# Tiles of the experts begin before the last batch's attention tail, whose pieces run between their products

## The chip, the cores and the metric

One core of one Trainium2 chip runs the whole kernel. The metric is the device time of one execution in microseconds. TensorE (PE) multiplies, VectorE (DVE) and ScalarE (ACT) do the elementwise work, GpSimd (POOL) does some of it and issues the indirect DMAs, SyncE (SP) issues the plain DMAs. Each engine runs its own program in order; they meet at semaphores.

## What is computed

8 batches of 512 tokens, width 256. Two layers, each followed by a layer norm over the sum with its input:

```
qkv = x @ qkv_w.T + qkv_b            # 16 heads of 16, causal softmax, attn @ v
mem_score ...                        # a decayed cumulative memory of 6x6 outer products per head
x1 = layernorm(x + (seq_out + gated * mem_val) @ out_w.T + out_b)
logits = x1 @ wr + br                # 4 experts, the best 2 per token
h = gelu(x1 @ w1[e] + b1[e]);  y = h @ w2[e] + b2[e]        # 256 -> 1024 -> 256
c[e] = gelu(b1[e]) @ w2[e] + b2[e];  c_sum = c.sum(experts)
out = layernorm(x1 + sum_k gate_k * (y[e_k] - c[e_k] + c_sum))
```

So a token's expert rows need only that token's x1 and routing; the constant rows c need weights alone.

## The kernel before, in words

**Attention.** `schedule` (L351) runs steps 0 to 9. In step i the scores, values and memory of batch i-1 run, the queries of batch i+1, and the tail of batch i-2: o_tokens, z, z_rows, projection, layernorm, seed, normalise, x1_rows, logits, gates, rank. Within a step every engine walks the same list of about 190 stage names, `stages_of_a_step` (L46), an order written out by hand, and does its own part of each stage. Step 8 (`B`) has no new queries, step 9 (`B + 1`) is the tail of the last batch alone. After `rank` POOL scatters each token's row of x1 (with its token number, its two gates and its expert) into `slots`, a region in DRAM for each expert, by 8 indirect DMAs a batch (L742). SP stores x1 in `sums` (L531).

**Weights of the experts.** 16 chunks of 128x1024 f32 come by 8 DMAs of 1 MB (L465). `weights(n)` turns a chunk into two f16 halves: ACT copies the high one (L805), DVE forms the low one (L1318). Chunks 0 to 5 are converted in step 8, chunks 6 to 15 in step 9.

**Constants.** In step 9 PE multiplies gelu(b1) with the f16 halves of w2 (`expert_of_nothing`, L1175, 96 matmuls); behind it DVE forms `c_all`, `c_sum` and `base` (L1631 to L1639).

**Table.** When all batches are ranked, DVE works out a table of 35 tiles of 256 rows (L1583 to L1626, some 40 small operations, most waiting for the one before): for each tile its expert, its first row in `slots` and how many rows to leave out. SP waits for all scatters and the table, then loads the rows of tiles 0 and 1.

**Tiles.** `ffn_schedule` (L364) runs tiles 0 to 35. In tile t PE does, for hc = 0 to 7, `first_layer(hc)` of tile t (6 matmuls, L1220) and `second_layer(hc)` of tile t-1 (6 matmuls, L1231); after hc 3 it transposes the rows of tile t+1 (`rows_of`, 4 transposes, L1208). ACT applies gelu (L949) and copies the transposed rows (`rows_high`, L940). DVE makes two f16 halves of each hidden block (L1681, L1683), at hc 4 the low half of the next tile's rows (`rows_low`, L1657), at hc 5 the bias (L1653), at hc 6 the gates (L1666 to L1674), and after hc 7 scales the output rows of tile t-1 (L1697, L1703), which POOL adds into `sums` (L767). `first_layer(hc)` waits for the gelu of four blocks before, a gelu for DVE's halves of four blocks before that; and PE may not begin tile t+1 before DVE has done `rows_low(t + 1)`, which stands behind hc 4 of tile t on DVE.

**End.** SP loads `sums`, DVE, ACT and POOL normalise, SP stores.

Of the kernel before, what the change touches and what calls it, by code (L numbers as in the profile page):

```python
# [13 lines left out]
P = 128  # L14
# [21 lines left out]
TABLE = TILES + 2  # L36
REGION = ROWS + N
# [4 lines left out]
RAW_B = range(4, 10)  # L42
# [69 lines left out]
def attention_and_ffn(nc, x_tok, x_tr, w_proj, qk_bias, v_bias, mem_bias, gate_bias, mem_scale, iter_mix, decay_logits, w_out,  # L112
                      out_bias, w_route, b_route, w_1, b_1, w_2, b_2, out):
    ctx = ExitStack()
    with ctx:
        sb = lambda name, shape, dt: ctx.enter_context(nc.sbuf_tensor(name, shape, dt))
        ps = lambda name: ctx.enter_context(nc.psum_tensor(name, [P, 512], F32))
        sem = lambda name: ctx.enter_context(nc.semaphore(name))
        dram = lambda name, shape, dt: nc.dram_tensor(name, shape, dt, kind="Internal").ap()


        q_rows = dram("q_rows", (2, 33, NP2, T), F16)
        k_rows = dram("k_rows", (2, 33, NP2, T), F16)
        decay_rows = dram("decay_rows", (H, 3 * P), F32)
        slots = dram("slots", (E * REGION, ROW), F32)
        sums = dram("sums", (N + ROWS, D), F32)


        def carve(arena, at, shape, dt):
# [31 lines left out]
        qk_parts, at = carve(arena_b, at, (4, 2, T), F16)  # L161
        v_aug, at = carve(arena_b, at, (C, H, 32), F32)
# [6 lines left out]
        w_raw_b, after_raw = carve(arena_b, after_probs, (len(RAW_B), CHUNK), F32)  # L169

        def raw_chunks(n, m=1):

            return w_raw_b[:, n - RAW_B[0]:n - RAW_B[0] + m, :] if n in RAW_B else w_raw[:, n:n + m, :]


        g_hi, g_lo, xt_hi, xt_lo, rows_x, y_out = ([None, None] for _ in range(6))
        at = 0
        for n in range(2):
            g_hi[n], at = carve(arena_b, at, (HC, ROWS), F16)
            g_lo[n], at = carve(arena_b, at, (HC, ROWS), F16)  # L180
# [173 lines left out]

        block = ctx.enter_context(nc.Block())

        stages = stages_of_a_step()

        def run(mine, i, ab, c, t):

# [66 lines left out]
        def _(sp):  # L427
# [80 lines left out]
            def step(i, par, ab, c, t):  # L508
# [32 lines left out]
                if ab:  # L541
# [3 lines left out]
                    if not later(i, 1):  # L545
                        tables()
# [1243 lines left out]
```

## Time and profile before

| what | us |
|---|---|
| runs | 1074.76, 1075.88 (median), 1081.32 |
| profiled execution, its own time | 1073.04 |
| its span, first to last instruction | 1071.3 |
| one attention step, from the stage table (steps 2, 4 and 5) | 68 |
| last matmul of the attention's values | 590.6 |
| first matmul of tile 0 | 640.81 |
| last matmul of the tiles | 1026.4 |
| busy PE, DVE, ACT, POOL | 938.2, 831.6, 490.4, 427.0 |

The times in rows are us from the start of the span. Matmuls are pipelined: in a run of them the start of the next is the better measure of what one costs than its own duration.

### The profile page before, as it was taken

The page shows a single profiled execution, that of the slowest core. Times are in us where ns is not written, and L with a number is a line of the kernel's source. Part 1 is how long each engine was busy: PE and PEld are TensorE (multiplying, and loading weights), DVE is VectorE, ACT ScalarE, POOL GpSimd, SP SyncE. Part 2 cuts the span into 40 slices and gives each one's busy share as a digit, 9 for nine tenths or more (in the row PEclk, how much of TensorE's full clock was granted, in tenths as well). Part 3 has the DMA queues.
Part 4 walks back from the last instruction along what each step waited for, and adds up shares of the span by engine and source line. Part 5 has one row for each costly group of instructions (what it writes and reads, how often), then busy time and mean ns, then how long its engine had stood idle before and what let it go on. Part 6 is the DMA issues. An engine that isn't in the chain of part 4 may idle for free.

```text
span 1071.3 us, 28021 instructions
## 1 busy us (share of the span) xinstructions
PE 938.2 (88%) x8034; PEld 688.5 (64%) x8035; DVE 831.6 (78%) x2944; ACT 490.4 (46%) x1038; POOL 427.0 (40%) x371
## 2 busy tenths in 40 slices
PE   4699999998999999998988749999999999999930
PEld 1155656565566565655645538888989889898920
DVE  4658798896988988978878867777777777777737
ACT  4174654554545555554555514333343334333304
POOL 8336084453553735636356131232323223232321
PEclk9699999999999999999999869999999999999975
DMA  4662124132032140320341311233332323232357
GB/s 161 180 179 71 32 62 120 41 91 94 22 110 91 60 121 1 105 76 21 125 192 41 118 61 32 41 55 44 50 48 49 49 49 49 49 49 42 53 114 234
DMA packets 60073, 85.19 MB, mean 80 GB/s; under 512 B 8473, under 2 KB 50985, under 8 KB 58953
## 3 DMA queue, kind: packets, MB, share of 16 engines
q1 hardware_dynamic: 45680, 62.20, 19.6%
q0 software_dynamic: 14304, 21.90, 11.1%
q8 instruction: 45, 0.74, 0.3%
q14 instruction: 44, 0.35, 0.1%
HBM read 48.08 MB, written 35.86 MB: 78 GB/s over the span
## 4 chain that ended last, share of the span: by engine, by line
PE 65%; DVE 17%; DMA 5%; issue 5%; SPq 2%; ACT 2%; POOL 2%; DVEq 1%; ACTq 0%; POOLq 0%
PE st L1220 8%; PE sm L1220 8%; PE pv L1231 8%; PE sm L1231 8%; PE ms L995 6%; PE sm L1077 5%; PE st L1037 4%; PE pv L1057 4%; DVE junk L1446 3%; PE ms L1135 3%; DVE beaten L1393 2%; PE ms L1107 2%; PE st L1039 2%; PE ms L1119 2%; PE ms L1208 2%
## 5 line engine op out<-in xcount | busy, mean ns | idle before, releaser
L1446 DVE CUSTOM_DVE_ANT_0 junk<-sm,mask_ts 128x512 bf16<-128x512 f32 (+3 forms) x512 | 220.3, 486 | 59.4 <-PE sm L1077 57.0
L885 ACT ACTIVATE arena_b<-st 128x512 f32<-128x512 f32 x320 | 181.7, 598 | 112.4 <-PE st L1039 111.1
L767 POOL DMA_INDIRECT sums<-arena_b x70 | 111.2, 1588 | 290.8 <-DVE arena_b L1703 253.0
L1037 PE MATMUL st<-arena_a 128*128 128x384 f16 (+3 forms) x512 | 127.8, 306 | 19.5 <-ACT arena_b L885 10.6
L1077 PE MATMUL sm<-arena_a 128*128 128x512 f16 (+3 forms) x512 | 115.2, 312 | 20.5 <-DVE maxes L1446 12.6
L1683 DVE TENSOR_TENSOR arena_b<-arena_b 128x256 f16<-128x256 f32 x280 | 119.7, 428 | 9.6
L949 ACT ACTIVATE arena_b<-st,arena_b 128x256 f32<-128x256 f32 x140 | 66.3, 473 | 116.7 <-PE st L1220 105.9
L949 ACT ACTIVATE arena_b<-sm,arena_b 128x256 f32<-128x256 f32 x140 | 66.3, 474 | 115.1 <-PE sm L1220 81.6
L1681 DVE CAST arena_b<-arena_b 128x256 f16<-128x256 f32 x280 | 87.7, 313 | 40.3 <-ACT arena_b L949 38.0
L1220 PE MATMUL st<-arena_b,arena_a 128*128 128x256 f16 x840 | 115.6, 275 | 1.8 <-DVE arena_b L1657 1.8
L1231 PE MATMUL pv<-arena_a,arena_b 128*128 x864 | 116.8, 273 | 0.0
L1220 PE MATMUL sm<-arena_b,arena_a 128*128 128x256 f16 x840 | 115.1, 274 | 0.0
L1231 PE MATMUL sm<-arena_a,arena_b 128*128 x816 | 111.3, 273 | 0.0
L742 POOL DMA_INDIRECT slots<-res,slot_i x64 | 65.8, 1028 | 105.9 <-DVE slot_i L1435 88.9
L1037 PEld LDWEIGHTS st<-arena_a 128*128 128x128 f16 x512 | 50.6, 99 | 74.5 <-ACT arena_b L885 27.5
L1039 PE MATMUL st<-mask_st,ident_b 128*128 128x128 bf16 x512 | 96.0, 221 | 0.0
L1231 PEld LDWEIGHTS pv<-arena_a,arena_b 128*128 128x128 f16 x864 | 84.4, 98 | 10.0
L1220 PEld LDWEIGHTS st<-arena_b,arena_a 128*128 x840 | 82.4, 98 | 12.2 <-issue 2.5
L1220 PEld LDWEIGHTS sm<-arena_b,arena_a 128*128 x840 | 82.6, 98 | 10.1
L1057 PE MATMUL pv<-arena_b 128*32 128x512 f32 (+3 forms) x1024 | 88.5, 447 | 0.0
L1231 PEld LDWEIGHTS sm<-arena_a,arena_b 128*128 128x128 f16 x816 | 79.8, 98 | 9.3
L1077 PEld LDWEIGHTS sm<-arena_a 128*128 128x128 f16 x512 | 41.8, 100 | 67.6 <-DVE maxes L1446 36.3
(253 smaller groups left out, 1657.1 us busy)
## 6 DMA issues: line engine op xcount, KB each, us to landing
arena_b<-slots SPq DMA_DIRECT2D x37, 260.0 KB, 2.7
arena_a<-w SPq DMA_DIRECT2D x5, 1024.0 KB, 8.5
arena_b<-x_tr SPq DMA_DIRECT2D x8, 512.0 KB, 3.7
q_rows<-arena_b SPq DMA_DIRECT2D x32, 128.0 KB
k_rows<-arena_b SPq DMA_DIRECT2D x32, 128.0 KB
arena_a<-q_rows SPq DMA_DIRECT2D x32, 128.0 KB
arena_a<-k_rows SPq DMA_DIRECT2D x32, 128.0 KB
res<-x_tok POOLq DMA_DIRECT2D x8, 512.0 KB, 4.0
```

Source lines behind the costliest of these rows:

```text
L767: pool.indirect_dma_start(sums, bass.IndirectOffsetOnAxis(ap=token_now[:, 1 - par, m:m + 1], axis=0), y_out[1 - par][:, m, :], None, compu ...
L885: act.activation(probs[:, q, :], st_ps[piece % 2][:, :], ACT.Exp, scale=SCORE_SCALE).then_inc(exp_done, 1)
L949: act.activation(g_32[:, hc % 4, :], u_bank(hc)[:, 0:ROWS], ACT.Gelu, bias=b1_now[:, par, hc:hc + 1], scale=1.0 / W_SCALE).then_inc(gelu_d ...
L1037: pe.matmul(out[:, at:at + width], ks[:, h % 2, h // 2, s * P:(s + 1) * P], qs[:, h // 2, s * P:T], start=m == 0, stop=False, skip_group_c ...
L1039: last = pe.matmul(out[:, at:at + P], ident_b[:, :], mask_st[:, :], start=False, stop=True, skip_group_check=True)
L1057: last = pe.matmul(out[32 * hl:32 * hl + 32, s * P:T], v_aug[:, s, 4 * g + hl, :], probs[:, slot, col:col + width], start=cls == 0, stop=c ...
L1077: last = pe.matmul(sm_ps[n % 3][:, at:at + width], qs[:, j, tile * P:(tile + 1) * P], ks[:, p, j, 0:width], start=m == 0, stop=True, skip_ ...
L1220: last = pe.matmul(u_bank(hc)[:, 0:ROWS], w_by_expert[:, up_expert, at:at + P], xs[par][:, kc, :], start=kc == 0 and n == 0, stop=kc == KC ...
L1231: last = pe.matmul(y_ps[1 - par][:, m * D:(m + 1) * D], gs[1 - par][:, hc, m * P:(m + 1) * P], w_by_expert[:, down_expert, at + lo * CHUNK ...
L1446: last = dve.tensor_tensor_reduce(junk[:, n % 3, at:at + width], sm_ps[n % 3][:, at:at + width], mask_ts[:, T - width:T], 1.0, NEG, ALU.ad ...
L1681: dve.tensor_copy(g_hi[par][:, hc, :], g_32[:, hc % 4, :]).then_inc(ghi_done, 1)
L1683: dve.tensor_tensor(g_lo[par][:, hc, :], g_32[:, hc % 4, :], g_hi[par][:, hc, :], ALU.subtract).then_inc(hid_done, 1)
```

## The change

- `stages_of_a_step` loses `weights`, `last_memory_scores` and step 9's four `nothing`, gains `load_w2`, `nothing`, `first_expert` and `first_rows`, and some 14 other stages stand one or two places from where they stood. Step 9 is no longer a step.
- Step 9's stages are dealt out by hand (`stages_of_the_tail`): two places in each of tiles 0 to 20. PE does its part after hc 1 and hc 5, ACT and DVE after hc 3 and hc 7, SP and POOL once a tile. All of the tail's PE stages use the one bank `ms1`.
- Constants: in step 0 ACT issues 8 DMAs (4 MB) of raw w2; in step 1 PE multiplies them in f32 with gelu(b1), 32 matmuls of 32 columns by 256, into `pv` (before the values), ACT copies, SP writes 4 rows to DRAM; in step 8 they are read back, and POOL forms `base` (5 operations) before the tiles.
- The table is made in three parts: 6 tiles in step 7 (`first_expert`: the most loaded expert after six batches has at least 1536 tokens, 6 tiles), tiles 6 to 24 in tiles 0 to 2 from the counts of seven batches, tiles 25 to 36 in tiles 18 to 20 from all counts. Experts are numbered from the most loaded one on, and their weights are fetched in that order.
- Weights: chunks 0 to 3 in step 8, chunks 4 to 15 in tiles 1 to 5. SP loads chunks 14, 15, 10 to 13 in step 8, chunks 4, 5 before tile 0, 6 to 9 in tiles 0 and 1.
- In step 0 SP sends the decays and the row of maxima before the rows of batch 1, where it sent them after.

```diff
+EARLY = (2 * (N - T) - E * (ROWS - 1) + ROWS - 1) // ROWS      # 25
+LATE = TABLE - EARLY                                           # 12
+UNROLLED = EARLY - 2                                           # 23
+SURE = 2 * (N - 2 * T) // E // ROWS                            # 6
...
+    tail = {
+        (0, 0): [("load_weights", 3)], (0, 1): [("early_table", 0)],
+        (1, 0): [("load_weights", 4), ("weights", 4), ("early_table", 1)], (1, 1): [("weights", 5)],
+        (2, 0): [("weights", 6), ("early_table", 2)], (2, 1): [("weights", 7), ("weights", 8)],
+        (3, 0): [("weights", 9), ("weights", 10)], (3, 1): [("weights", 11)],
+        (4, 0): [("weights", 12), ("weights", 13)], (4, 1): [("weights", 14)],
+        (5, 0): [("weights", 15)], (5, 1): [("last_memory_scores", 0)],
+        (6, 0): [("o_tokens", 0)], (6, 1): [("o_tokens", 1), ("last_memory_gates", 0)],
+        (7, 0): [("o_tokens", 2), ("last_gates", 0)], (7, 1): [("o_tokens", 3), ("z", 0)],
+        (8, 0): [("z_rows", 0), ("z", 1)], (8, 1): [("z_rows", 1), ("z", 2)],
+        (9, 0): [("z_rows", 2), ("z", 3)], (9, 1): [("z_rows", 3)],
+        (10, 0): [("projection", 0)], (10, 1): [("projection", 1)],
+        (11, 0): [("projection", 2)], (11, 1): [("projection", 3)],
+        (12, 0): [("layernorm", 0)], (12, 1): [("layernorm", 1)],
+        (13, 0): [("seed", 0)], (13, 1): [("layernorm", 2), ("layernorm", 3)],
+        (14, 0): [("normalise", 0), ("normalise", 1)], (14, 1): [("normalise", 2), ("normalise", 3)],
+        (15, 0): [("x1_rows", 0), ("store", 0)], (15, 1): [("x1_rows", 1)],
+        (16, 0): [("x1_rows", 2)], (16, 1): [("x1_rows", 3)],
+        (17, 0): [("logits", 0)], (17, 1): [("gates", 0)],
+        (18, 0): [("rank", 0)], (18, 1): [("late_table", 0), ("scatter", 0)],
+        (19, 0): [("late_table", 1)], (19, 1): [("late_table", 2)], (20, 0): [("late_table", 3)], (20, 1): [("late_table", 4)],
+    }
...
-            step(B + 1, 1, False, False, True)
-        def ffn_schedule(eng, tile):
-            tile(0, 0, True, False)
-            tile(1, 1, True, True)
-            tile(2, 0, True, True)
-            with eng.Fori(0, (TILES - 3) // 2) as k:
+        def tail(mine, t, point):
+            for stage, n in tail_stages.get((t, point), ()) if isinstance(t, int) else ():
+                if stage in mine:
+                    mine[stage](n)
+        def ffn_schedule(eng, tile, before_late):
+            for t in range(UNROLLED):
+                tile(t, t % 2, True, t > 0)
+            before_late()
+            with eng.Fori(0, (TILES - UNROLLED) // 2) as k:
...
+            def base_of_experts():                       # POOL, ahead of the tiles
+                pool.wait_ge(base_in, 32)
+                pool.tensor_tensor(b2_all, b2_all, base, ALU.add).then_inc(base_chain, 1)
+                for e in range(1, E):
+                    pool.wait_ge(base_chain, e)
+                    pool.tensor_tensor(c_sum, b2_all[:, 0, :] if e == 1 else c_sum, b2_all[:, e, :], ALU.add).then_inc(base_chain, 1)
+                pool.wait_ge(base_chain, E)
+                pool.tensor_tensor(base, c_sum.unsqueeze(1).broadcast_to([P, E, D]), base, ALU.subtract).then_inc(base_done, 1)
...
+            def load_w2(_):                              # ACT, step 0
+                act.wait_ge(rows_in[0], 16 * N_ROWS_IN)
+                for e in range(E):
+                    for n in range(2):
+                        act.dma_start(w2_raw[2 * e + n], w_2[e, :, n, :].rearrange("p (a t) -> p a t", a=2)).then_inc(w2_in, 16)
...
+                    pe.wait_ge(w2_in, 32 * E)            # PE, step 1, behind ("scores", 3)
+                    pe.wait_ge(gb_done, 1)
+                    pe.wait_ge(bias_done, 1)
+                    for hc in range(HC):
+                        for e in range(E):
+                            rows = w2_raw[2 * e + hc // 4][:, hc % 4 // 2, D * (hc % 2):D * (hc % 2) + D]
+                            last = pe.matmul(pv_ps[32 * e:32 * e + 32, 0:D], gb[:, HC * e + hc:HC * e + hc + 1].broadcast_to([P, 32]), rows,
+                                             start=hc == 0, stop=hc == HC - 1, skip_group_check=True)
...
+                if isinstance(i, int) and i == B + 1:    # PE: bank()
+                        n = 1
...
                 if up:                                   # PE: tile()
                     pe.wait_ge(xt_lo_s, n_of(t + 1))
+                    if not later(t, 1):
+                        pe.wait_ge(wlo_done, CHUNKS)
+                    elif not later(t, SURE + 1) and later(t, SURE):
+                        pe.wait_ge(wlo_done, CHUNKS * E)
...
+                    if up and hc in (1, 5):
+                        tail(mine, t, hc // 4)
...
+            pe.wait_ge(table_done, 3)
+            pe.wait_ge(exp_done, 40 * B)
+            pe.wait_ge(mrow_done, 2 * B)
...
+                        if hc in (3, 7):                 # DVE and ACT: tile()
+                            tail(mine, t, hc // 4)
```

## Rows read from the trace of the kernel before

**Rows 1.** The page: busy us of each engine, share of the span, instructions.

```profile
PE 938.2 (88%) x8034; PEld 688.5 (64%) x8035; DVE 831.6 (78%) x2944; ACT 490.4 (46%) x1038; POOL 427.0 (40%) x371
```

**Rows 2.** Stage table: stretch, length, busy of PE, PEld, DVE, ACT, POOL, clock, DMA.

```profile
528.00:594.00 66.00, 55.34 (x484) 35.51 (x483) 54.84 (x163) 38.03 (x82) 36.38 (x29) 0.97 0.39 145
594.00:641.00 47.00, 26.13 (x163) 20.01 (x164) 35.19 (x112) 16.56 (x28) 10.11 (x9) 0.72 0.20 67
...
800.00:900.00 100.00, 100.00 (x918) 89.96 (x917) 76.80 (x257) 39.07 (x83) 28.64 (x18) 1.00 0.30 48
```

**Rows 3.** PE in order of time: start, length, line; last values, first tiles.

```profile
589.09 1.50 PE L1057 MATMUL pv<-arena_b 128*32 128x384 f32 x24
...
640.81 2.74 PE L1220 MATMUL st<-arena_b,arena_a 128*128 128x256 f16 x12 [1.61 <-DVE arena_b L1657]
...
665.98 0.60 PE L1208 MATMUL ms<-ident,arena_b 128*128 128x128 f32 x4
666.41 0.82 PE L1220 MATMUL st<-arena_b,arena_a 128*128 128x256 f16 x6
```

**Rows 4.** DVE groups, 700 to 1000 us: busy, mean ns, idle before and releasers.

```profile
L1681 DVE CAST arena_b<-arena_b 128x256 f16<-128x256 f32 x220 | 69.0, 314 | 28.6 <-ACT arena_b L949 26.9
...
L1653 DVE COPY arena_b<-b_all 128x8 f32 x28 | 4.9, 174 | 14.2 <-ACT arena_b L949 8.2 <-issue 5.9
```

**Rows 5.** In order of time: DVE's `rows_low(3)`, and PE's first matmul of tile 3.

```profile
668.45 0.68 DVE L1657 TENSOR_TENSOR arena_b<-ms,arena_b 128x512 f16<-128x512 f32 x1
...
671.65 0.82 PE L1220 MATMUL st<-arena_b,arena_a 128*128 128x256 f16 x6
```

**Rows 6.** DVE in order of time, 589 to 629 us: the tail's pieces.

```profile
589.45 0.56 DVE L1499 TENSOR_TENSOR mr<-rdm,lines 128x384 f32<-128x384 f32 x1
...
593.03 0.23 DVE L1519 TENSOR_SCALAR sg<-sg 128x128 f32<-128x128 f32 x1
...
593.80 0.25 DVE L1526 RECIPROCAL rec<-ms 128x16 f32<-128x16 f32 x1
...
596.58 0.22 DVE L1550 TENSOR_SCALAR sg<-sg 128x128 f32<-128x128 f32 x1
...
598.64 1.67 DVE L1538 SCALAR_TENSOR_TENSOR zs<-mv_odd,gated,zs 128x256 f32<-128x256 f32 x4
...
616.83 0.17 DVE L1388 TENSOR_TENSOR lg<-ms,b_r 128x16 f32<-128x16 f32 x1
...
620.59 0.17 DVE L1435 CAST slot_i<-slot_k 128x8 int32<-128x8 f32 x1
620.67 2.35 DVE L1318 SCALAR_TENSOR_TENSOR arena_a<-arena_a 128x1024 f16<-128x1024 f32 x2
622.95 0.16 DVE L1583 TENSOR_TENSOR count<-first_free,first_slot 128x4 f32<-128x4 f32 x1
...
628.87 0.24 DVE L1626 CAST arena_b<-arena_b 128x37 int32<-128x37 f32 x1
```

**Rows 7.** POOL, and DVE, in order of time: a DVE operation beside a POOL addition.

```profile
571.34 2.37 POOL L727 TENSOR_TENSOR mv_odd<-mv_odd,mem_b 128x1024 f32<-128x1024 f32 x1
...
571.41 2.32 DVE L1393 TENSOR_TENSOR beaten<-lg 128x8 f32<-128x8 f32 x1
```

**Rows 8.** ACT in order of time: the load of gelu's table.

```profile
620.99 1.28 ACT L934 ACT_TABLE_LOAD   x1
```

**Rows 9.** Chain of waits: start, us, what: PE's projection and logits of a tail.

```profile
503.61 1.75 PE ms L1152 x16
...
547.23 2.72 PE ms L1135 x12
```

**Rows 10.** PE in order of time: step 1's first scores; 8 matmuls of 32 columns.

```profile
53.91 0.61 PE L1037 MATMUL st<-arena_a 128*128 128x512 f16 x1 [4.29 <-DMA arena_a<-max_row]
...
563.06 0.64 PE L1057 MATMUL pv<-arena_b 128*32 128x256 f32 x8
```

**Rows 11.** The page's DMA issues: size, median us from issue to landing.

```profile
arena_a<-w SPq DMA_DIRECT2D x5, 1024.0 KB, 8.5
```

More of the change, by code:

```diff
@@ L529, in step @@
                     b = i - 2
[L530 to L531 removed]
+                    store(b, par)
+                if ab and not later(i, 1):
+                    decays_out()
+                    max_rows_in(i, par, 0)
+                    decays_in()
                 if ab and before_end(i, 1):
@@ L573, in tile, with before_late @@
                     sp.wait_ge(row_info, n_of(t + 1))
+                    if not later(t, SURE - 1) and later(t, SURE - 2):
+                        sp.wait_ge(scattered, 128 * (B - 1))
+                        sp.wait_ge(table_done, 6)
                     load_rows(t + 2, par)
-            load_rows(0, 0)
-            load_rows(1, 1)
-            ffn_schedule(sp, tile)
+                    tail(mine, t, 0)
+            def before_late():
+                sp.wait_ge(scattered, 128 * B)
+                sp.wait_ge(table_done, 9)
+            sp.wait_ge(st_ready, 40 * B)
+            load_weights(2)
+            mine = {"load_weights": load_weights, "store": lambda _: store(B - 1, 1)}
+            ffn_schedule(sp, tile, before_late)
             for n in range(2):
@@ L976, in queries_and_keys, with rows_of @@
                 last.then_inc(qk_ready, 1)
+            def rows_of(t, par):
+                if not later(t, 1):
+                    pe.wait_ge(cs_read, 6 * B - 1)
+                pe.wait_ge(rows_x_in[par], n_of(16 * half(t) + 16))
+                if later(t, 1):
+                    pe.wait_ge(xt_lo_s, n_of(t))
+                for kc in range(KC):
+                    for m in range(2):
+                        last = pe.transpose(ms_ps[0][:, kc * ROWS + m * P:kc * ROWS + (m + 1) * P], rows_x[par][:, m, kc * P:(kc + 1) * P], ident[:, :])
+                last.then_inc(xt_ready, 1)
             def step(i, par, ab, c, t):
@@ L1224, in second_layer @@
                 def second_layer(hc):
+                    if hc == 0 and not later(t, 2):
+                        pe.wait_ge(o_evac, 4 * B)
                     if hc == 0 and later(t, 3):
@@ new lines, in tiles_of, with starts_of @@
+            def tiles_of(out, rows, more_rows):
+                f(dve.tensor_scalar(n_tok, rows, more_rows, None, ALU.add))
+                f_wait()
+                f(dve.tensor_scalar(n_int, n_tok, ROWS.bit_length() - 1, None, ALU.arith_shift_right))
+                f_wait()
+                f(dve.tensor_copy(out, n_int))
+                f_wait()
+            def starts_of(tiles):
+                f(dve.memset(starts[:, 0:1], 0.0))
+                f(dve.tensor_copy(starts[:, 1:2], tiles[:, 0:1]))
+                f_wait()
+                for e in range(1, E):
+                    f(dve.tensor_tensor(starts[:, e + 1:e + 2], starts[:, e:e + 1], tiles[:, e:e + 1], ALU.add))
+                    f_wait()
@@ new lines, in by_position, with positions @@
+            def by_position(out, n, first, steps):
+                f(dve.tensor_scalar(out, past[:, 0, 0:n], steps[:, 0:1], first, ALU.mult, ALU.add))
+                f_wait()
+                for e in range(1, E - 1):
+                    f(dve.scalar_tensor_tensor(out, past[:, e, 0:n], steps[:, e:e + 1], out, ALU.mult, ALU.add))
+                    f_wait()
+            def positions(at, n, now):
+                for e in range(E - 1):
+                    f(dve.tensor_scalar(past[:, e, 0:n], now, starts[:, e + 1:e + 2], None, ALU.is_ge))
+                f_wait()
+                f(dve.tensor_tensor(tab_f[:, 3, at:at + n], past[:, 0, 0:n], past[:, 1, 0:n], ALU.add))
+                f_wait()
+                f(dve.tensor_tensor(tab_f[:, 3, at:at + n], tab_f[:, 3, at:at + n], past[:, 2, 0:n], ALU.add))
+                f_wait()
@@ L1689, in tile @@
                             row_gates()
+                        if hc == 3 and not later(t, SURE) and later(t, SURE - 1):
+                            dve.wait_ge(table_done, 6)
+                        if hc in (3, 7):
+                            tail(mine, t, hc // 4)
                 if down:
                     dve.wait_ge(y_ready, n_of(t))
+                    if not later(t, 2):
+                        dve.wait_ge(base_done, 1)
                     if later(t, 3):
```

462 lines of the change are left out of this document (289 added, 173 removed).

## The prediction

> **What bounds the kernel now.** I read the page's busy shares first: PE is busy 88% of the span, DVE 78%, so PE leads and DVE is close behind [rows 1]. The stage table says where PE isn't the bound: in the steady tiles PE is busy 100 of 100 us at the full clock of 2.4 GHz; between the attention and the tiles it is busy 26 of 47 us, at a granted clock of 0.72 [rows 2]. PE in order of time gives the edges of that stretch: the last values end at 590.6, tile 0 begins at 640.81 [rows 3]. In it stand the last tail (a chain from engine to engine), the conversion of ten weight chunks, the constants, the table, the last scatter and the first loads. This stretch is what the change opens. Then I asked the tiles how much room there is for what is put between them. A tile is 100 matmul records and 918 start in 100 us, so 10.9 us [rows 2]. DVE's idle time waiting for ACT is 26.9 + 8.2 us in 300 us, 27.5 tiles: 1.3 us a tile [rows 4]. The rest of what looks idle on DVE is issue of instructions (gaps ahead of the bias and of the output rows), shorter where tiles are written out, so I take 1.5 us of real room and 9.4 us of DVE work a tile. And the nearest deadline is tight: `rows_low(3)` ends at 669.13, PE begins tile 3 at 671.65 [rows 5]. DVE may be late by 2.5 us at that place; every further us holds PE.
>
> **The sum.** It starts at the profiled execution's own time, 1073.0; the median of the runs, 1075.9, lies 2.8 above it, and I add that at the end.
>
> *Tiles start earlier.* PE needs the last exponentials, the expert of tile 0 and the first four chunks, all of step 7 or 8, so tile 0 begins about 0.3 us behind the values: 590.9 for 640.81, -49.9.
>
> *Start-up of the tiles.* A group of four transposes holds PE for 0.43 (665.98 to 666.41, [rows 3]), so a group of six matmuls takes (10.9 - 0.43) / 16 = 0.65. From 640.81 the transposes inside tile 2 should come after 2.6 + 8.3 + 10.9 us, at 662.6; they stand at 665.98. The first 12 matmuls of tile 0 took 2.74 instead of 1.3 us, the half clock of 1.2 GHz behind a long gap; the rest was waits. With no gap both go: -3.3.
>
> *PE's share of the tail* now lies in the tiles, where PE is full, so it counts whole. 32 f32 transposes, 0.43 for four: 3.5. The projection, 16 matmuls at 2.72 for 12: 3.6; the logits 1.75 [rows 9]; rank 0.3. Together +9.1. The 96 matmuls of the constants are gone with the gap.
>
> *Tiles 0 to 5, DVE.* Prices [rows 6]: one low half of a chunk 2.35 / 2 = 1.17; the last memory scores 589.45 to 593.26, 3.8; a chained small operation: 5.92 us from 622.95 for about 33 rows, 0.18. The three early tables are about 12, 9 and 8 such operations, the first with a register load (one such gap is up to 0.6): 2.7, 1.9, 1.6. DVE's work is then, tile by tile: 7.8 (no output rows yet) + 2.7 = 10.5; 9.4 + 2.3 + 1.9 = 13.6; 9.4 + 3.5 + 1.6 = 14.5; 12.9; 12.9; 9.4 + 1.2 + 3.8 = 14.4. Sum 78.8. ACT first has to load gelu's table (1.28, [rows 8]), so DVE starts 2.4 us behind PE. `rows_low(6)` stands 8.9 us ahead of the end of that sum, so PE begins tile 6 at 2.4 + 78.8 - 8.9 = 72.3 us from the start of tile 0. PE alone would be there after 5.7 (tile 0 has a first layer only) + 5 x 10.9 = 60.2. **Stall: +12.1.** This is the largest term against the change: what hid DVE in the tiles was 1.5 us a tile, and 4.1 a tile are put on it.
>
> *Base on POOL.* Five additions, two of 1024 elements (2.37 each, [rows 7]) and three of 256, about 6.5 us around 595 to 602, in tiles 0 and 1. A DVE operation of 8 elements with both operands in SBUF took 2.32 beside such an addition [rows 7]; the tail's small ones, with POOL idle, take 0.16 to 0.25 [rows 6]. The halves L1681 and L1683 read and write SBUF, so they should be held too. Bounds: 0 to 6.5; as DVE is the bound there and still gets an operation in between, I take +4.5.
>
> *Tiles 6 to 8.* DVE comes into tile 6 late, and the tail's PE stages share one bank: `o_tokens(1)` (after hc 5) waits until DVE has read `o_tokens(0)` (after its hc 3). DVE is there at 81.2 (the whole sum) + 2.7 (four blocks) + 0.65 (reciprocal 0.25 and product 0.42, rows 6) = 84.6, PE at 72.3 + 0.4 + 8.3 = 81.0: 3.6. Tile 7 puts 0.65 + 2.06 (the gates, 596.58 to 598.64) and 1.05 on DVE; `z_rows(0)` comes another 0.5 late. +4, bounds 1 and 7. From tile 9 to 16 DVE's pieces are below 2 us a tile, and PE's own pieces give room: 0.
>
> *Tiles 17 to 21.* Logits and rank are 3.9 us on DVE (616.83 to 620.76, rows 6), in tiles that PE lengthens by 1.75. Then five parts of the late table, about 2.4, 1.6, 2.1, 1.9, 1.2, stand in two and a half tiles with 1.5 us of room each, plus the 2.5 of the deadline: +3, bounds 1 and 6.
>
> *ACT.* Three places need Exp or Ln between gelus, six table loads: 7.7 us at 1.28 [rows 8]. A pair (away from gelu and back) and its operations take about 3 us, and PE asks for that gelu four blocks later; at tile 13 the delayed `rows_high` just meets the deadline: 0, at most +2. The Trainium skill (ScalarE: Activation LUTs, What ACT_TABLE_LOAD costs) states that a switch costs as much again in a drain, 2.66 us; by that the pair would be 5.3 and tile 13 about 2.5 us late, and the sum 2.5 higher. The row's next operation starts 0.02 us behind the load, so the trace does not show the drain.
>
> *Steps 0 to 8.* The constants are 32 matmuls of 256 f32 columns, four side by side; 8 such held PE for 0.57 [rows 10], so 2.3 at full clock, 4.6 at half. They wait for 4 MB; 1 MB landed after 8.5 us [rows 11] and ACT issues them some 20 us ahead, beside the tiny row of maxima for which PE waited 4.29 us [rows 10]. That row is now sent about 1.5 us sooner. Net +1.5, bounds -1.5 and +8. `first_expert` puts about 16 chained operations on DVE in step 7, 3 us: +1, bounds 0 and 3. The moved stages: PE is not busy for 10.7 of the 66 us of step 8 [rows 2], so a better or worse order can give or take about 1 us a step; I take 0, bounds -4 and +4. The scatter (8 indirect DMAs on POOL in tile 18), the store and the row loads on SP have a tile or more of slack behind them: 0. Chunks 4 and 5 are issued behind 2 MB at 590 and wanted at 603: at most 8.5 each, in parallel, 0, bound +5.
>
> Sum: 1073.0 - 49.9 - 3.3 + 9.1 + 12.1 + 4.5 + 4 + 3 + 1.5 + 1 = **1055.0**, and with 2.8 **1057.8** as a median. Forecast: 1058.
>
> **Rivals.**
> *DVE takes it in.* If the small operations and gaps overlap when DVE runs behind, and POOL holds nothing, the 23.6 us of stalls shrink to 5: 1039. For it: no row shows DVE working off a backlog longer than one tile's end. Against it: a work sum of 78.8 us in 60 us leaves at least 12 less what overlaps. 12%.
> *The gain is spent on waits that I priced at nothing.* A stall of ACT for chunks 4 to 9 (SP may issue 6 and 7 only behind `row_info` of tile 1, then 8.5 us), the 4 MB in front of the row of maxima, a worse order. Price: 5 + 8 + 4 on top, 1065 to 1075, no change that can be told. 14%.
> *Slower: the clock falls with the stalls.* PE waits about 2.5 us at the head of each of tiles 1 to 8. In the gap of now the granted clock was 0.72 for a busy share of 26 in 47, in step 8, with 55 of 66 busy, 0.97 [rows 2]; tiles with 20% waiting lie like step 8. Were the clock at 1.2 GHz for all of tiles 0 to 8, their 93 us would be 186, less the 20 of stalls that this would hide: 1131. It takes about 36 us at half clock, beyond those that fill stalls, to lose the whole gain. 4%.
> *It doesn't start early.* SP's program of step 8 is one line of waits (constants written, scatters of six batches, table) ahead of the rows of tile 0; if one came late, tile 0 would wait. All of them are met by 575 to 580; each us late costs one us. 2%.
>
> **How the numbers follow.** My case, stalls of 14 to 32 us, has 68%: 1047 to 1067. The range goes down half way to the first rival and up to where the second has most of its weight: 1043 to 1072. What a measurement here can tell from no change is about 1%, 10.8 us: faster is below 1065.1. My case but its upper twelfth and the first rival make 0.74 for faster, the second rival and that twelfth 0.20, the clock and the rest 0.06.
>
> **What would show it.** The trace of after should have the first L1220-like matmul near 591; PE waits for `rows_low` (DVE) at the head of tiles 1 to 6, about 2 us each; DVE busy over 90% from 593 to 670 with f16 halves stretched to 2 us around 598; tile 6 near 668; waits of the tail's transposes for DVE in tiles 6 and 7; free running from 9 to 17; a few us of waits in 19 to 21. The term most likely off is POOL's. If DVE turns out to run below 90% in tiles 1 to 5 while PE waits, another engine or a load is late and my mechanism is wrong.

## The result

| | median us | runs | ratio to the kernel before, 95% interval |
|---|---|---|---|
| before | 1077.38 | 4 | |
| changed | 1065.18 | 4 | 0.988 [0.985, 0.991] |
| changed, measured again | 1061.14 | 5 | 0.983 [0.981, 0.986] |

The forecast was 1058, range 1043 to 1072. The change makes the kernel 1.2 to 1.7% faster, its time is 7 us above the forecast in the first series and 3 in the second, in which the kernel before had 1078.09 (9 runs). The profiled execution of the changed kernel took 1066.83, its span is 1065.1.

The page of the changed kernel, busy us of each engine, answers to [rows 1]: PE has 9 us less than before (the constants alone are busy for 5.1 us instead of 12.4), DVE 3 us more.

```profile
PE 929.2 (87%) x8002; PEld 676.0 (63%) x8003; DVE 835.0 (78%) x2990; ACT 495.6 (47%) x1045; POOL 430.5 (40%) x376
```

The stage table of the changed kernel, columns as in [rows 2]:

```profile
528.00:594.00 66.00, 56.20 (x490) 34.90 (x490) 51.92 (x160) 36.75 (x82) 33.82 (x28) 0.97 0.29 101
594.00:641.00 47.00, 40.47 (x353) 33.08 (x352) 37.11 (x114) 23.12 (x44) 16.72 (x14) 0.93 0.45 152
641.00:700.00 59.00, 53.74 (x470) 46.43 (x468) 53.24 (x156) 28.90 (x52) 16.40 (x10) 0.97 0.29 46
800.00:900.00 100.00, 95.23 (x869) 84.49 (x867) 79.91 (x305) 38.73 (x80) 36.00 (x26) 1.00 0.34 63
```

Between 594 and 641 PE now does 40.5 us of work instead of 26.1: the gap is full. But from 641 to 700 it is busy for only 53.7 of 59 us, and DVE for 53.2, that is 90%. The steady tiles of [rows 2], 100 of 100, have become 95 of 100 where pieces of the tail lie between them.

PE in order of time (the number in brackets is its idle time ahead and what ended it), the end of the attention and the head of tiles 0 and 1; it answers to [rows 3]:

```profile
599.77 1.50 PE L1222 MATMUL pv<-arena_b 128*32 128x384 f32 x24
...
601.45 1.48 PE L1375 MATMUL st<-arena_b,arena_a 128*128 128x256 f16 x12 [0.17 <-issue]
...
604.08 0.60 PE L1138 MATMUL ms<-ident,arena_b 128*128 128x128 f32 x4
...
612.46 1.46 PE L1375 MATMUL st<-arena_b,arena_a 128*128 128x256 f16 x6 [5.16 <-DVE arena_b L1659]
613.71 1.49 PE L1388 MATMUL pv<-arena_a,arena_b 128*128 x6
...
616.27 1.49 PE L1388 MATMUL pv<-arena_a,arena_b 128*128 x6
617.55 0.96 PE L1375 MATMUL sm<-arena_b,arena_a 128*128 128x256 f16 x6
618.35 0.82 PE L1388 MATMUL pv<-arena_a,arena_b 128*128 x6
...
696.67 0.60 PE L1138 MATMUL ms<-ident,arena_b 128*128 128x128 f32 x4
```

Tile 0 starts 0.2 us behind the last values, at 601.45 instead of 640.81. Then tile 1's first product waits 5.16 us for `rows_low(1)`. Behind that wait six matmuls take 1.46 to 1.49 us instead of 0.82: the engine is back at 1.2 GHz for four groups (the granted clock from 609 to 620 is 0.69). Their pitch is 1.28 instead of 0.65, so the wait costs 2.5 us more than its length.

What PE waited for between 594 and 860, in the changed kernel (us in total, times, longest):

```profile
PE ms L1138 <- DMA arena_b<-slots: 7.2, 8, 1.9
PE st L1375 <- DVE arena_b L1659: 6.9, 3, 5.2
PE ms L1284 <- DVE zs L1862: 2.4, 1, 2.4
```

The forecast had only the second and third. The first is the load of a tile's rows; whether it is a cause of its own is what one of the experiments asks. DVE and POOL behind tile 0, the lines that answer to [rows 7]:

```profile
602.37 2.35 POOL L798 TENSOR_TENSOR arena_b<-arena_b 128x1024 f32<-128x1024 f32 x1
604.80 2.39 POOL L801 TENSOR_TENSOR arena_b<-arena_b 128x256 f32<-128x256 f32 x3
607.27 2.40 POOL L803 TENSOR_TENSOR arena_b<-arena_b 128x1024 f32<-128x1024 f32 x1
```

```profile
603.85 1.03 DVE L1940 CAST arena_b<-arena_b 128x256 f16<-128x256 f32 x1 [3.87 <-ACT arena_b L1099]
...
607.40 2.42 DVE L1940 CAST arena_b<-arena_b 128x256 f16<-128x256 f32 x1
609.86 0.42 DVE L1942 TENSOR_TENSOR arena_b<-arena_b 128x256 f16<-128x256 f32 x1
610.20 0.29 DVE L1940 CAST arena_b<-arena_b 128x256 f16<-128x256 f32 x1
```

A cast of 0.29 us takes 2.42 beside POOL's last addition. The first three blocks take 603.85 to 610.20, 6.35 us, where three free ones take 2.0.

**Four lengths** serve for all comparisons below, since a start that is late by chance drops out of them. *Step 1*: from the first to the second transposes of maxima. *Attention*: from the first of these to the end of the last values. *Tiles 1 to 8*: from the transposes inside tile 0 to those inside tile 7 (604.08 to 696.67 here, 92.6; free of waits and of the tail's pieces it would be 73.8, since half of the first of these seven spans belongs to tile 0, which has no second layer: 8.3, then six times 10.9). The *tile phase* runs from tile 0's first product to the end of the last first-layer product.

| us | step 1 | attention | tiles 1 to 8 | tile phase |
|---|---|---|---|---|
| before, its two traces | 32.0, 35.1 | 542.0, 545.3 | 75.1, 75.1 | 379.7, 379.6 |
| changed, its two traces | 38.3, 36.7 | 549.6, 550.2 | 92.6, 92.4 | 411.7, 409.6 |

### The profile page after: what moved, and what is told of

Its sections match the earlier page's. It is cut to its first block, busy times and chain, and to the rows that moved or that the text cites. A ratio compares the mean times of both kernels' runs of the same rounds, so it can differ in the third digit from the quotient of the medians.

```text
span 1065.1 us, 26698 instructions
## 1 busy us (share of the span) xinstructions
PE 929.2 (87%) x8002; PEld 676.0 (63%) x8003; DVE 835.0 (78%) x2990; ACT 495.6 (47%) x1045; POOL 430.5 (40%) x376
## 4 chain that ended last, share of the span: by engine, by line
PE 55%; DVE 25%; issue 6%; DMA 6%; SPq 4%; ACT 2%; DVEq 1%; POOL 0%; ACTq 0%; POOLq 0%
PE sm L1375 6%; PE st L1375 5%; PE ms L1160 5%; PE sm L1388 5%; PE pv L1388 5%; PE sm L1242 5%; PE st L1202 4%; PE pv L1222 4%; DVE junk L1780 4%; PE ms L1300 3%; DVE arena_b L1942 3%; DVE arena_b L1940 2%; PE ms L1272 2%; DVE beaten L1727 2%; PE st L1204 2%
## 5 line engine op out<-in xcount | busy, mean ns | idle before, releaser
L1242 PE MATMUL sm<-arena_a 128*128 128x512 f16 (+3 forms) x512 | 112.9, 309 | 18.0 <-DVE maxes L1780 11.9
L792 POOL DMA_INDIRECT slots<-res,slot_i x64 | 62.5, 977 | 80.2 <-DVE slot_i L1769 62.8
L1242 PEld LDWEIGHTS sm<-arena_a 128*128 128x128 f16 x512 | 41.6, 99 | 63.1 <-DVE maxes L1780 35.1
```

The source lines that it names most:

```text
L1242: last = pe.matmul(sm_ps[n % 3][:, at:at + width], qs[:, j, tile * P:(tile + 1) * P], ks[:, p, j, 0:width], start=m == 0, stop=True, skip_ ...
```

## The experiments

**The control.** The changed kernel, no edit.

> The changed kernel as it is, as the measure for the three that run beside it. 1065 us, within 0.3%. Its trace of before the experiments has: values end at 601.3 us, tile 0's first product at 601.45, 25 us of waits of PE in the tiles. If the step markers (end of the last maxima of each step) stand at other places than 124.7, 193.6, 265.3, ..., part of the 8 us by which steps 0 and 1 came later is scatter between executions.

Measured: 1061.14 (5 runs), span 1064.0. The values end at 602.51, tile 0's first product is at 602.69. The marker of step 1 stands at 89.0 here and at 90.0 in the other trace, so most of the lateness stays, and where it stands moves by a microsecond or two between executions.

**The kernel before, once more,** to see how far its start moves.

> The kernel before, unchanged, for a second trace of it. The first transposes of maxima stood at 48.6 in its first trace and at 47.1, 47.7, 48.5, 51.0, 51.5, 51.6, 51.7, 52.3 and 52.5 in nine traces of the changed kernel and its variants. If that is scatter of the start in both kernels, this one stands anywhere between 47 and 53; if the changed kernel starts later as such, at 48.6 or less.

Measured: 1079.34. The lines of its trace for the two marks of step 1 and for tile 0's first product:

```profile
50.67 0.60 PE L1092 MATMUL sm<-ident,maxes 128*16 128x128 f32 x2 [1.40 <-DVE maxes L1446]
...
85.76 0.39 PE L1092 MATMUL sm<-ident,maxes 128*16 128x128 f32 x2 [0.44 <-DVE maxes L1446]
...
647.25 2.74 PE L1220 MATMUL st<-arena_b,arena_a 128*128 128x256 f16 x12 [1.61 <-DVE arena_b L1657]
```

The start is scatter in both kernels, up to 5 us between executions. The trace from which I forecast was an early one: tile 0 stood at 640.81 in it, at 647.25 in this one. The tile phase is the same to 0.1 us (379.7, 379.6).

**The tail in front of the tiles.** All five engines run the pieces of the tail before tile 0:

```
 def ffn_schedule(eng, tile, before_late, mine={}):
+    for at in sorted(tail_stages):
+        for stage, n in tail_stages[at]:
+            if stage in mine:
+                mine[stage](n)
```

> All pieces of the last batch's tail, the remaining conversions and the tables are run before tile 0 instead of between the products of tiles 0 to 20; nothing else is changed. It undoes the one part that the forecast makes the gain of. Theory: tile 0's first product starts 40 to 50 us later than 601, at 643 to 652; in the tiles DVE and PE have no extra work, so the 25 us of waits and the 9 us of PE's pieces go; 1065 + 45 - 25 - 9 = about 1076, no better than the kernel before. Rival (the earlier tiles are not worth their price, most of the gain over the kernel before comes from the other edits): below 1066.

Measured: 1115.19. PE in order of time:

```profile
666.59 3.55 PE L1319 MATMUL ms<-w_r,z_t 128*128 128x4 f32 x16 [0.56 <-ACT z_t L1010]
671.46 0.20 PE L1328 MATMUL ms<-taken,before 128*128 128x16 bf16 x1 [1.32 <-DVE taken L1734]
...
671.70 2.52 PE L1377 MATMUL st<-arena_b,arena_a 128*128 128x256 f16 x11
...
687.69 1.46 PE L1377 MATMUL st<-arena_b,arena_a 128*128 128x256 f16 x6 [8.44 <-DVE arena_b L1661]
...
1061.80 0.82 PE L1377 MATMUL sm<-arena_b,arena_a 128*128 128x256 f16 x6
```

Tile 0 starts at 671.70, 69 us later than the control's, not 40 to 50: the tail works with one bank of PSUM here, and DVE converts all twelve chunks before it (of PE's 45 us of waits, 29.5 are one wait for DVE). The tile phase is 390.9, 18.7 us shorter than the control's. It has a stall of its own at its head: DVE is still at the ranks and the late table when PE begins tile 0, and PE waits 8.4 us for `rows_low(1)`. From the transposes inside tile 1 to the end of the phase it takes 367.5, where the control takes 390.8 and the kernel before 365.5. So both halves of the trade are shown: between the products the pieces cost the tiles 19 us in all and 23 from tile 1 on, and not having them in front is worth more, 50 us less in the whole span of the two traces. The two sizes are those of this arrangement of the tail, which is worse than that of the kernel before with its gap of 50 us.

**POOL's additions moved into step 8.**

```
 (POOL, step 8)
+    if isinstance(i, int) and i == B:
+        base_of_experts()
     scatter(i, par)
 (POOL, behind step 8)
-    base_of_experts()
```

> The five additions for the base are moved on POOL from behind the scatter of step 8 (602.4 to 609.7) into POOL's idle time ahead of it (585.0 to 592.4); nothing else is changed. Theory (POOL's additions hold DVE's operations with SBUF operands, and DVE's lateness in tiles 0 to 5 passes to PE one for one): DVE's first three blocks take 2.0 us instead of 6.35, PE's waits in tiles 0 to 5 fall from 13.4 to about 9, and the kernel is 3.5 to 4.5 us faster than the control. Rival A (PE in tiles 2 to 5 waits for row loads and ACT, not for DVE's sum of work): the gap at tile 1 closes and comes back by tile 6, 0 to 1 us faster. Rival B: in step 8 the additions hold DVE's choice of experts or the memory's products instead; then the values end later than 601.3 by 2 to 4 us and the gain is gone.

Measured: 1062.53, ratio 0.986 [0.983, 0.988], no better than the control. Its trace shows why: tiles 1 to 8 take 86.3 (control 92.4), tile phase 404.2 (409.6), but from the transposes of maxima in step 8 to the last values it takes 41.0 instead of 37.2. Rival B: 5.4 us gained in the tiles, 3.8 lost in step 8. One line of DVE and one of POOL of this kernel:

```profile
586.39 1.95 DVE L1733 TENSOR_SCALAR taken<-place 128x16 bf16<-128x16 f32 x1
```

```profile
585.97 2.34 POOL L798 TENSOR_TENSOR arena_b<-arena_b 128x1024 f32<-128x1024 f32 x1
```

In the control that operation takes 0.17. It stands in the chain that chooses the experts, for which the memory's products wait.

**The base on 128 x 8 elements.** SP loads the rows of the constants spread over all partitions, POOL adds there, SP writes the base out and loads it broadcast in step 8:

```
+for q in range(E):
+    for to, of in ((small_b, b_2), (small_c, c_rows)):
+        sp.dma_start(to[32*q:32*q+32], AP(of, ap=[[8, 32], [D, E], [1, 8]]))   # end of step 6
-pool.tensor_tensor(b2_all, b2_all, base, ALU.add)        # 128x1024
+pool.tensor_tensor(small_b, small_b, small_c, ALU.add)   # 128x32, step 7
...
+sp.dma_start(base_rows, small_own)                       # step 8, then one broadcast load
```

> The base is computed in step 7 on 128 partitions x 8 elements (five additions of 8 to 32 elements instead of 256 to 1024), written to DRAM and loaded broadcast in step 8, so POOL adds nothing at 602 to 610 and nothing extra in step 8. Theory (moving the additions into step 8 gained 5.4 us in the tiles and lost 3.8 in step 8, because they held DVE there): now the 5.4 to 6 us of tile 1 are gained and step 8 stays at 37.2 us from its last transposes of maxima to the last values; tile phase 404 us, end 5 us earlier. Rival (step 8 in the moved kernel was longer by scatter or by something else than POOL's additions): step 8 is longer here too.

Measured: 1053.46 in one run. POOL and PE of this kernel:

```profile
511.46 0.26 POOL L813 TENSOR_TENSOR small_b<-small_b,small_c 128x32 f32<-128x32 f32 x1
511.80 0.76 POOL L816 TENSOR_TENSOR small_b<-small_b 128x8 f32<-128x8 f32 x3
512.64 0.20 POOL L818 TENSOR_TENSOR small_own<-small_b,small_own 128x8 f32<-128x8 f32 x1
```

```profile
604.03 0.83 PE L1391 MATMUL st<-arena_b,arena_a 128*128 128x256 f16 x6 [0.79 <-DVE arena_b L1675]
...
686.01 0.60 PE L1154 MATMUL ms<-ident,arena_b 128*128 128x128 f32 x4
```

The wait at tile 1 falls from 5.16 to 0.79 and the six matmuls behind it take 0.83: no half clock. Tiles 1 to 8 take 86.0 (600.02 to 686.01), the tile phase 402.4, and the last part of step 8 stays at 37.0. The term that I called "base on POOL" is 6.4 to 7.2 us: 4.4 of held DVE, and the rest mostly the clock behind the wait. The whole time of this single run is flattered by an early start (its first mark stands at 48.5).

**DVE without the low halves of chunks 4 to 15.**

```
+if n >= CHUNKS:
+    dve.memset(w_ffn[:, at + CHUNK:at + 2 * CHUNK].bitcast(F32), 0.0)
+    return
 dve.scalar_tensor_tensor(w_ffn[:, at + CHUNK:at + 2 * CHUNK], ...)
```

> DVE clears the low halves of chunks 4 to 15 instead of computing them (the products of the other experts lack that part): 12 instructions of 1.22 us become 12 of some 0.3, so DVE has 11 us less in tiles 1 to 5, all else alike. Theory (DVE's sum of work sets PE's waits in tiles 0 to 5): DVE's work per tile falls to about 10 to 11.5, PE's waits in tiles 0 to 8 fall from 18.0 to 7 or 8, 9 to 11 us faster than the control. Rival (row loads, issued by SP only after DVE's gates of the rows at the end of a tile and landing some us later, or ACT): waits for rows stay as they are, 3 us faster or less.

Measured: 1055.6 (6 runs), ratio 0.981 [0.978, 0.983]. DVE's groups between 605 and 690, of the changed kernel and of this one (instructions | busy us, mean ns):

```profile
L1485 DVE SCALAR_TENSOR_TENSOR arena_a<-arena_a 128x1024 f16<-128x1024 f32 x12 | 14.4, 1218 | 0.2 <-ACT arena_a L942 0.2
```

```profile
L1486 DVE MEMSET arena_a<- 128x512 f32 x12 | 5.8, 485 | 1.4 <-ACT arena_a L942 0.9
```

DVE saved 12 x (1.218 - 0.485) = 8.8 us, and waited 1.2 us more for ACT (1.4 for 0.2), 7.6 net. Tiles 1 to 8 went from 92.4 to 83.6, by 8.8, but 1.4 of that lies ahead of the transposes of tile 1, before the first changed instruction (614.39); from there on it is 76.2 against 68.8, 7.4. So DVE's work is passed on nearly one for one, and this is the plainest proof that its sum sets this stretch. The medians differ by 5.5 us (1061.14 and 1055.60), less than the 9 to 11 that I expected: clearing was dearer than the 0.3 us that I had put.

**The row gates earlier,** for the loads of rows that PE waited for.

```
 if hc == 4:
     rows_low(t + 1, 1 - par)
+    row_gates()
-if hc == 6:
-    row_gates()
```

> DVE computes the rows' gates behind hc 4 of a tile instead of behind hc 6, so SP issues the load of the rows for two tiles on some 2.5 us earlier; DVE's work is the same. Theory as predicted (DVE's sum of work sets tiles 1 to 5): PE's waits for rows turn into waits for DVE, tile phase changes by less than 1.5 us. Rival (the row load is a chain of its own, DVE's gates, SP, DMA, PE, and set tiles 2 to 5 and 21): spacings of tiles 2 to 8 (12.4, 13.2, 11.7, 11.4, 15.8 in the control) fall together by 3 to 6 us, and the waits for row loads vanish.

Measured: 1082.2, the slowest of the tile variants. The waits for row loads are gone, and tiles 1 to 8 take 94.4 (92.4): what PE had waited for the DMA it now waits for DVE, here 8.5 us for `rows_low` instead of 6.9, and 4.2 instead of 2.3 for `zs`. So the loads were only the messenger of DVE's lateness. The tile phase, however, is 423.2, 13.5 us longer, where I had expected less than 1.5 of change. Most of it is a new price, in the tiles from 25 on, which were free and now take about 12.0 instead of 10.9. DVE's waits from 900 to 1000 us:

```profile
DVE arena_b L1925 <- DMA sums<-arena_b: 16.5, 8, 2.2
```

`row_gates` has to wait for the write-back of the tile before, which lands 2 us later than hc 4, and the gelu halves queue behind it.

**The conversions spread evenly,** one to a half tile.

```
-(2, 1): [("weights", 7), ("weights", 8)],  (3, 0): [("weights", 9), ("weights", 10)], ...
+(0, 1): [("early_table", 0), ("weights", 4)],  (1, 0): [..., ("weights", 5), ...],  (1, 1): [("weights", 6)], ...
+(5, 0): [("weights", 13)],  (5, 1): [("weights", 14), ("weights", 15), ("last_memory_scores", 0)],
```

> The twelve conversions of chunks 4 to 15 stand one to a half tile from the second half of tile 0 to tile 5 instead of up to two in the halves of tiles 1 to 5; DVE's work up to tile 6 is the same. Theory (the sum of DVE's work up to the deadline counts, not its peaks): tiles 1 to 6 together take the same to 1 us, but earlier tiles are held longer. Rival (peaks count, since in light tiles the lateness is made good): 3 to 5 us faster in tiles 1 to 6.

Measured: 1060.65 (one run). Tiles 1 to 8 take 93.2 (92.4): two of them now run free (10.9 and 11.0), and one takes 18.7, where PE waits for the last conversion, with the half clock behind it:

```profile
671.21 1.46 PE L1375 MATMUL st<-arena_b,arena_a 128*128 128x256 f16 x6 [4.43 <-DVE arena_a L1485]
```

The sum counts, not the peaks.

**Without the constants.** The 4 MB of second matrices and 28 of the 32 matmuls left out.

> The load of the second matrices in step 0 (4 MB) and 28 of the 32 matmuls of the constants in step 1 are left out (the result for an expert of nothing is wrong). Theory (the constants are the term that I priced too low: 4.8 us of PE at half clock, waits behind them in step 1, and the late read of the constants by ACT at 85 us): the marker of step 1 comes 6 to 8 us earlier than the control's, and so does the end: 1058. Rival (the later start of PE, 18.7 for 15.9 us, and the other order of the stages made the 8 us): 0 to 2.5 us faster.

Measured: 1063.56, ratio 0.986 [0.984, 0.989]: nothing gained, step 1 takes 38.4. The expectation failed, and the rival names no cause. PE in order of time, and ACT:

```profile
59.58 0.72 PE L1339 MATMUL pv<-w_o,gb 128*32 128x256 f32 x8
...
86.66 0.50 PE L1202 MATMUL st<-arena_a 128*128 128x384 f16 x1 [6.17 <-ACT arena_b L1028]
```

```profile
77.94 0.61 ACT L1028 ACTIVATE arena_b<-st 128x512 f32<-128x512 f32 x1
85.52 0.60 ACT L1040 ACTIVATE o_t<-pv 128x512 f32<-128x512 f32 x1 [6.97 <-DMA c_rows<-o_t]
```

PE begins the next products (`values_in`) 7.7 us behind the first mark instead of 10.4 and 11.9 in the two traces of the changed kernel, and then gives 3.7 us back in one wait (6.17 for 2.43 and 2.49). ACT's first values out overwrite the place of the constants' rows, so ACT stands for 7 us until SP's write of them has landed, its exponentials queue behind, and PE queues behind those. SP sends that write behind the twenty loads of batch 1's rows. With the matmuls in, ACT stands for 3.2 and PE for 2.4 us of it.

**The constants' rows written first.**

```
 const_row_of_keys(1)
+c_rows_out()
 rows_from_dram(i + 1, 1 - par, 0)
```

> SP writes the four rows of the constants to DRAM ahead of batch 1's row loads (in its idle time at 64 to 69 us) instead of behind them; nothing else is changed. Theory (ACT must not overwrite the constants before SP has written them out, ACT's first values out in step 1 wait for it, its exponentials queue behind, and PE waits: 2.4 us in the control, 6.2 us with the constants' matmuls left out): the wait of PE for ACT near 86 us goes, the stretch between the first two transposes of maxima (36.7 to 38.4 us in the four traces, 32.0 in the kernel before) falls to 34 to 35, and the rest stays. Rival (the other order of the stages makes step 1 longer): the stretch stays at 36.7 or more.

Measured: 1065.49 in one run. SP's queue:

```profile
64.14 1.08 SPq L548 DMA_DIRECT2D c_rows<-o_t  x4
69.32 0.31 SPq L602 DMA_DIRECT2D arena_a<-q_rows  x1
```

The wait is gone (0.2 us of waits for ACT instead of 2.6), step 1 takes 35.1 instead of 36.6 to 38.4 in the nine other traces with the new order of the stages and the write behind the loads. The attention, 547.8 instead of 549.6 and 550.2, proves nothing by itself: `weights_even`, with the wait still in, has 547.8 too. The single time doesn't show the gain either: the rest of this execution has 412 in its tile phase.

**The stages in the order of before.**

> The stages of the eight steps stand in the order of the kernel before, with the new ones (constants, first expert, first rows) at their new places. Theory as predicted (the order is worth nothing): the stretch from the third transposes of maxima to the fifteenth (412.0 us in the kernel before; 413 to 415 in six traces of the changed one) and step 8 stay within 1.5 us. Rival (the new order costs in steps 2 to 7): 412 again, and step 1 shorter than 36.7 too.

Measured: 1061.93 (one run). From the third transposes of maxima to the fifteenth it takes 414.4 (changed 413.1 and 415.0, before 412.0 and 410.9), and the whole attention 549.0. So the order costs nothing that I could find in steps 2 to 7. Step 1, however, takes 34.9: with the old order the first values out come at 79.71, after the write of the constants has landed by itself, and ACT doesn't wait. The new order had only uncovered that wait.

**All together,** with the tail's pieces one tile later from the last memory scores on.

```
-(5, 1): [("last_memory_scores", 0)], (6, 0): [("o_tokens", 0)], ...
+(6, 1): [("last_memory_scores", 0)], (7, 0): [("o_tokens", 0)], ...
```

> The constants' rows written first, the base computed on 128 x 8 elements in step 7, and every piece of the last batch's tail from the last memory scores on put one tile later (they end in tile 21 instead of 20). From the single edits: 1.6 to 3 us in step 1, 7 us in tiles 1 to 8; from the third, the last memory scores (3.8 us of DVE's work) leave the sum of tiles 0 to 5, and DVE has tile 6 to make its lateness good before the pieces that share one bank begin. Theory (DVE's sum up to tile 6 and the shared bank set tiles 1 to 8): base_small's 86.0 us from tile 0's transposes to tile 8's (rows_of 1 to 8) fall by another 3 to 5, the waits of tiles 17 to 21 only move on by a tile; 1050 us, ratio to the kernel before 0.973 to 0.978. Rival (lateness then comes up in tiles 7 to 9 instead): the third edit gives 0 to 1, ratio 0.978 to 0.981.

Measured: 1055.46 (6 runs), ratio 0.980 [0.977, 0.983]; the control has 0.983 [0.981, 0.986]. The two intervals overlap, so that it beats the changed kernel is likely, not shown. Its trace is 11 us shorter than the control's at nearly the same start (first mark 51.4 and 52.3): step 1 34.3, attention 547.5, tile phase 402.0. Over the 402.4 of the base alone, the later tail gives 0.4. In tiles 1 to 9 it gains 2.1, and 1.7 comes back by the end: the rival was right in substance, the lateness moves on.

## Why the prediction was right, and where it was off

**Tile 0 starts with the end of the attention: right.** 0.2 us behind the last values. The gap that it closed was 50.2 us in one trace of before and 51.3 in the other.

**The tile phase: right in sum, and in part by luck.** Start-up, PE's share and the four kinds of stalls came to -3.3 + 9.1 + 12.1 + 4.5 + 4 + 3 = +29.4. Measured, the tile phase grew from 379.7 and 379.6 to 411.7 and 409.6, by 29.9 to 32.2. But the terms were off in both directions: DVE's too large by 3.8, POOL's and ACT's too small by some 2 each, as the next paragraphs say, and the three misses nearly cancel.

**DVE's sum in tiles 0 to 5: the mechanism right, the size too large.** From tile 0's first product to the transposes inside tile 5 a free run takes 54.6 us. The changed kernel takes 67.9 and 67.8, so 13.3 of stalls where I had 12.1 + 4.5 = 16.6; with POOL's additions made small it takes 62.9, 8.3 where I had 12.1. DVE was busy there (597.4 to 666) for 60.8 of 68.6 us, and I had counted 69.9 of work up to that place, issue gaps included; that fewer gaps count when DVE is behind is likely and not shown. I had named DVE below 90% in tiles 1 to 5 as the sign of a wrong mechanism; it was 91% (55.1 of 60.4 us from 609.0 to 669.4), just on the right side. Three runs bear on the mechanism: 7.6 us less work is 7.4 us less time, moving work between these tiles changes little (93.2 for 92.4), and what looks like waits for row loads is the same lateness on another path (94.4). I had not named that path: DVE's gates, SP, the DMA, PE. The bare length of these waits made it look like the larger cause; the experiment says that it isn't one.

**Base on POOL: the mechanism right, the size short.** I took 4.5 within 0 to 6.5; it is 6.4 to 7.2. DVE was held by 4.35 us as priced. What I left out is that a single long wait of PE is followed by a stretch at 1.2 GHz, 2.5 us more. My rival of a falling clock had it over all of tiles 0 to 8, at 73 us net; it exists, for a few groups behind single waits. The Trainium skill ("SBUF — State Buffer", "Who interferes with whom") says that `copy`, `cast` and `tensor_scalar`, where their operands meet certain conditions, and an operation with two inputs in SBUF beside a GpSimd instruction that reads SBUF, can be held by GpSimd for the whole of its instruction; the traces agree, with 2.42 for a cast of 0.29 and 1.95 for a `tensor_scalar` of 0.17. In the forecast I had argued from one row with two SBUF operands; the page would have told me that the casts, with one, can be held as well, which I had only assumed.

**Tiles 6 to 8 and 17 to 21: right within their bounds.** Beyond free tiles and PE's own pieces they cost 4.4 to 4.6 (I had 4) and 3.6 to 4.9 (I had 3). The one wait for `zs` is 2.4 us, and the later tail did not remove more than 2.1.

**ACT: short by 2.0 to 2.5.** I took 0, at most +2, and counted a pair of loads for each leaving of gelu. ACT of the changed kernel in tile 13:

```profile
767.63 1.28 ACT L984 ACT_TABLE_LOAD   x1
768.92 0.21 ACT L984 ACTIVATE rs<-rs 128x4 f32<-128x4 f32 x1
769.15 1.28 ACT L986 ACT_TABLE_LOAD   x1
770.44 0.20 ACT L986 ACTIVATE rs<-rs 128x4 f32<-128x4 f32 x1
770.66 1.28 ACT L1099 ACT_TABLE_LOAD   x1
771.96 0.47 ACT L1099 ACTIVATE arena_b<-st,arena_b 128x256 f32<-128x256 f32 x1
```

The logarithm and the exponential behind it take a load each, so gelu is away for 4.3 us instead of 3, and the tile, in which PE has no extra piece, takes 13.4 (control 12.9) instead of 10.9: PE waits 0.6 us for a gelu and 1.0 to 1.5 for the next rows. The drain of another 1.38 us behind each load, which the Trainium skill states ("ScalarE: Activation LUTs", "What ACT_TABLE_LOAD costs"), does not show here either: the next operation starts 0.01 to 0.02 us behind.

**The step that failed is "Steps 0 to 8".** I had +1.5 for the constants and +1 for `first_expert`, bounds -1.5 to +8 and 0 to 3. Measured, the attention is 549.6 and 550.2 instead of 542.0 and 545.3: between 4.3 and 8.2 longer, in the middle 6.3, so some 3.8 us more than the 2.5. Step 7 has 1.5 to 1.7 of it (32.9 us between its marks instead of 31.4 and 31.2), though the stretches on both sides of it are 1.0 shorter together. Most of the rest is in step 1, 4.0 us in the middle, of which the next stretch gives 0.9 back; two traces of the kernel before, 32.0 and 35.1, leave a wide margin around it. The constants' matmuls hold PE for 3.6 to 5.0 us in the eleven traces that have them, mostly 4.8 to 5.0, a little above the 4.6 that I had as the price at half clock; against them I set the row of maxima, sent earlier, which is real (PE waits 2.7 to 3.1 instead of 4.3 and 6.5). What I had no term for is the wait of ACT for the write of the constants' rows behind SP's twenty loads: 3.2 us in the control, 2.4 of them passed on to PE. I had listed what the change puts into SP's queue in step 8, and not what it puts at the end of the queue in step 0 with a reader's place waiting for it.

**The base of the sum** was one execution with an early start: its tile 0 stood 6.4 us before that of the second trace. That is in the distance between the sum and the median, and no fault of a step.

The rival "gain spent on waits priced at nothing" named three causes: the chunks for ACT, the 4 MB in front of the row of maxima, a worse order. None of the three shows in the traces: PE waits less for the row of maxima than before, ACT shows no wait for a chunk from 580 to 700, and the order of before gained nothing. Its band, from 1065, begins where the first series lies, by a cause that it did not have.

## What to carry to other kernels

Work put between the products of a busy engine costs what it makes the second busiest engine late, added up until the next deadline. It is enough to sum up that engine's work up to there; how it is spread changed nothing here, and a sum taken from busy time and issue gaps of other tiles came out too high. A wait that PE shows for a DMA can be the lateness of another engine, passed on through a queue. Before a transfer is put at the end of a queue, ask who needs the place that it reads from, and when.

And an operation that contends is cheaper made small than moved: elsewhere it held another chain and gave back 3.8 of the 5.4 us that it had gained.

## What the runs showed of the hardware

- After a wait of 4.4 to 8.4 us between dense tiles PE ran its next two to four groups of six matmuls at 1.2 GHz (1.46 to 1.49 us instead of 0.82), which cost 1.3 to 2.5 us and did not grow with the wait (2.5 behind 5.2 us, 2.2 behind the 8.4 of the tail in front). Behind waits of 2.3 to 2.4 us for `zs` it happened in some traces (the changed kernel, 687.28) and not in others (the small base), and behind 0.8 us not. The Trainium skill ("TensorE: Matmul & The Clock Gate", "HAM oscillation — how this bites in real kernels") describes the same in a matmul kernel whose waits between bursts let each burst start at the lower clock; the traces agree.
- POOL's additions on 128 x 1024 elements (2.3 to 2.4 us) held single DVE operations for as long as themselves: a cast with one SBUF input (2.42), an operation with two (2.32, [rows 7]), a `tensor_scalar` on 16 elements (1.95). The same sums on 128 x 8 to 128 x 32 elements took 0.2 to 0.26 us.
- Clearing 128 x 512 f32 took DVE 0.485 us.
- The same program reached its first transposes of maxima anywhere from 47.1 to 52.5 us, over twelve traces of the changed kernel and its variants and two of the kernel before. One trace is not enough to say where a kernel's first 50 us went.
